# Graph attention on one core: sixteen late key tiles in place of twelve, every block of them moved by DMA, and a new order of PE's work in a step

## The reference

```
h = relu(layernorm(x))
q, k, v = h @ Wq[head], h @ Wk[head], h @ Wv[head]            # per head, 4096 x 64
scores = q @ k.T / 8 + 0.01 * eye - 1e16 * (1 - max(adj, eye))
out = x + sum over heads of softmax(scores) @ v @ Wo[head]
```

## Time and profile before

| what | value |
|---|---|
| time, median of three runs | 3127.58 us |
| span of the profiled execution | 3131.2 us |
| PE busy | 3056.8 us (98%) |
| DVE busy | 2444.3 us (78%) |
| ACT busy | 2171.6 us (69%) |
| POOL busy | 492.8 us (16%) |
| TensorE granted clock, mean | 0.992 |

### The profile page before, as it was taken

The page is one execution under the profiler, slowest core; times in us unless marked ns, Lnnn a source line. Parts: engine busy times, 40 slices in busy tenths (PEclk is TensorE's granted clock), DMA queues, the critical chain, the costliest instruction groups (busy, mean ns, idle before and its releaser), DMA issues.

```text
span 3131.2 us, 58791 instructions
## 1 busy us (share of the span) xinstructions
PE 3056.8 (98%) x18368; PEld 1892.8 (60%) x18368; DVE 2444.3 (78%) x4345; ACT 2171.6 (69%) x3297; POOL 492.8 (16%) x658
## 2 busy tenths in 40 slices
PE   7999999999999999999989999999999999999998
PEld 5566666666666666666556655666665666565664
DVE  6778788887878887887557877878877778777775
ACT  3677777777777777777547767767777667677675
POOL 3011111101111110111001111111111111111110
PEclk9999999999999999999999999999999999999999
DMA  5234444433444443344424433444433444433442
GB/s 154 53 85 88 95 79 98 84 81 78 91 91 84 94 85 85 73 95 87 94 74 80 88 84 73 87 93 81 93 79 72 86 94 81 93 79 72 89 93 52
DMA packets 217847, 267.82 MB, mean 86 GB/s; under 512 B 57472, under 2 KB 176768, under 8 KB 217728
## 3 DMA queue, kind: packets, MB, share of 16 engines
q1 hardware_dynamic: 173568, 178.51, 24.6%
q0 software_dynamic: 41984, 83.91, 16.1%
q10 hardware_dynamic: 2176, 4.19, 0.4%
HBM read 169.87 MB, written 12.71 MB: 58 GB/s over the span
## 4 chain that ended last, share of the span: by engine, by line
PE 92%; DVE 3%; issue 3%; DMA 1%; SPq 1%; DVEq 0%; ACT 0%; POOL 0%; POOLq 0%
PE psS L383 31%; PE psO L406 23%; PE psT L396 21%; PE psO L417 10%; PE psP L368 2%; PE psS L341 2%; DVE S L631 1%; PE psP L426 1%; PE psO L356 1%; PE psP L356 1%; DVE PT L645 1%; DMA S<-in_x 1%; SPq L239 0%; DMA S<-hT_scratch 0%; PE psT L327 0%
## 5 line engine op out<-in xcount | busy, mean ns | idle before, releaser
L631 DVE CUSTOM_DVE_ANT_0 S<-psS,B 128x1024 f32<-128x1024 f32 x1024 | 1239.6, 1211 | 169.0 <-PE psS L383 151.5
L517 ACT ACTIVATE S<-S,negm 128x1536 f32<-128x1536 f32 (+1 forms) x768 | 1094.8, 1427 | 62.9 <-DVE negm L638 59.7
L524 ACT ACTIVATE PT<-psT 128x512 f32<-128x512 f32 x768 | 457.0, 595 | 656.0 <-PE psT L396 654.3
L406 PE MATMUL psO<-PT,V 128*64 128x256 f32 x5120 | 836.0, 405 | 0.0
L396 PE MATMUL psT<-ident,S 128*128 128x128 f32 x5120 | 797.6, 283 | 31.4 <-DVE PT L645 24.3
L396 PEld LDWEIGHTS psT<-ident,S 128*128 128x128 f32 x5120 | 566.2, 141 | 398.2 <-issue 293.6
L383 PE MATMUL psS<-K,QH 128*128 128x512 f32 x2048 | 738.3, 442 | 8.4 <-DVE mx L631 5.9
L383 PE MATMUL psS<-K,QL 128*128 128x512 f32 x2048 | 643.8, 395 | 0.0
L645 DVE COPY PT<-psT 128x512 f32<-128x512 f32 x512 | 352.7, 689 | 332.4 <-PE psT L396 292.1
L658 DVE STREAM_TRANSPOSE S<-S 128x1536 f32<-128x1536 f32 x256 | 454.0, 1773 | 38.0 <-PE psO L417 37.9
L406 PEld LDWEIGHTS psO<-PT,V 128*64 128x64 f32 x5120 | 254.1, 135 | 362.4 <-issue 248.6
(11 more groups left out here) (52 smaller groups left out, 1056.1 us busy)
## 6 DMA issues: line engine op xcount, KB each, us to landing
S<-S SPq DMA_DIRECT2D x1536, 96.0 KB, 2.2
B<-in_adj POOLq DMA_DIRECT2D x256, 256.0 KB, 5.4
hq<-hT_scratch SPq DMA_DIRECT2D x32, 256.0 KB, 3.2
RB<-rden_scratch SPq DMA_DIRECT2D x128, 64.0 KB, 3.2
S<-in_x SPq DMA_DIRECT2D x8, 512.0 KB, 3.6
hT_scratch<-S ACTq DMA_DIRECT2D x8, 512.0 KB, 4.1
acc<-in_x POOLq DMA_DIRECT2D x16, 256.0 KB, 4.5
partial_scratch<-res POOLq DMA_DIRECT2D x16, 256.0 KB, 3.2
```

What stands on the lines that cost most here:

```text
L406: last = nc.tensor.matmul(psO[a * KD:(a + 1) * KD, 0:QW], V[:, 2 * s + a, h * KD:(h + 1) * KD], PT[:, s % RING, a * QW:(a + 1) * QW], star ...
L517: nc.scalar.activation(part, part, ACT.Exp, bias=negm[:, h % 2, q:q + 1], accum_out=sums[:, h % 2, q, e:e + 1]).then_inc(probs_ready, 1)
L524: nc.scalar.activation(PT[:, s % RING, :], psT[s % 2][:, :], ACT.Copy).then_inc(pt_act, 1)
L631: nc.vector.tensor_tensor_reduce(out=part, in0=psS[j % 2][:, :], in1=B[:, q, k * SLOT:(k + 1) * SLOT], scale=SCALE, scalar=LOWEST, op0=ALU ...
```

## The change

- `LATE` goes from 12 to 16, so the early key tiles go from 20 to 16: `TS` from 10 slots to 8, `SUBSTEPS` from 5 to 4. Each late transpose is 2048 columns wide instead of 1536, each move carries 2048-byte rows instead of 1536-byte ones, and `T1(h)` now fills all 4096 columns of query tile 1 in the other half. The first slot that waits for `late_moved` is slot 4 instead of slot 5 (`t1_first_slot`).
- All 16 quadrant blocks are moved by SP's DMAs (`MOVES` = 16); ACT's `copy_late` is gone.
- ACT takes all 8 slots; DVE takes none.
- PE's substep is: transposes 2c, transposes 2c + 1, scores c + 2, values 2c - 2, values 2c - 1. After the four substeps: scores 6, values 6 and 7, scores 7, late values of 6 tiles, scores 0 of the head after next, late values of 10 tiles, scores 1 of the head after next.
- DVE's list: mask 2, 3 and 4 in substeps 1, 2 and 3, then mask 5, then (even steps) both `query_lo`, then masks 6 and 7. The denominators stay in substep 2, ahead of mask 4.
- At the change of group, SP's weight loads also wait for the very last late values.

```diff
-LATE = 12
+LATE = 16
-MOVES = QUAD * (QUAD - 1)
+MOVES = QUAD * QUAD
-ACT_SLOTS = [0, 2, 4, 6, 8, 9]
-DVE_SLOTS = [1, 3, 5, 7]
+LATE_SPLIT = 6
+def t1_first_slot():
+    return SPT + (N - QT * LATE * P) // SLOT
 # wait_taken
-        slots, taken, start = (ACT_SLOTS, pt_act, PT_START) if s % TS in ACT_SLOTS else (DVE_SLOTS, pt_dve, 0)
-        engine.wait_ge(taken, count(i, h, len(slots), slots.index(s % TS) + 1 + start - (len(slots) if s < 0 else 0)))
+        engine.wait_ge(pt_act, count(i, h, TS, s + 1 + PT_START))
 # sync_program, at the change of group
         load(0, 0)
+        if not norm:
+            sp.wait_ge(late_used_before, STEPS)
 # sync_program, step
                 for qj in range(QUAD):
-                    if qi != qj:
-                        src, dst = late_blocks(h, qi, qj)
-                        sp.dma_start(dst, src).then_inc(late_moved, 16)
+                    src, dst = late_blocks(h, qi, qj)
+                    sp.dma_start(dst, src).then_inc(late_moved, 16)
 # tensor_program, step
             for c in range(SUBSTEPS):
                 transposes(i, h, 2 * c)
+                transposes(i, h, 2 * c + 1)
                 if nxt:
                     scores(i1, h1, c + 2)
...
                 if c:
                     values(i, h, 2 * c - 2)
-                transposes(i, h, 2 * c + 1)
-                if c:
                     values(i, h, 2 * c - 1)
...
             if nxt:
+                scores(i1, h1, SLOTS - 2)
+            values(i, h, TS - 2)
+            values(i, h, TS - 1)
+            if nxt:
                 scores(i1, h1, SLOTS - 1)
-            values(i, h, TS - 2)
+            values_late(i, h, range(LATE_SPLIT))
             if nxt2:
                 scores(i2, h2, 0)
-            values(i, h, TS - 1)
-            values_late(i, h)
+            values_late(i, h, range(LATE_SPLIT, LATE))
             if nxt2:
                 scores(i2, h2, 1)
 # scalar_program, step
-                if c in (1, 2):
-                    copy_late(i, h, (2 * c - 2, 2 * c - 1))
-                if 2 * c + 1 in ACT_SLOTS:
-                    take_slot(i, h, 2 * c + 1)
+                take_slot(i, h, 2 * c + 1)
 # vector_program, mask
-            if j == SPT + 1 and not first:
+            if j == t1_first_slot() and not first:
                 dve.wait_ge(late_moved, count(i, h, 16 * MOVES, 0))
-                dve.wait_ge(late_copied, count(i, h, QUAD, 0))
 # vector_program, step
-                if 2 * c + 1 in DVE_SLOTS:
-                    take_slot(i, h, 2 * c + 1)
...
-                if nxt2 and h % 2 == 0 and c > QUERY_AT:
-                    query_lo(i2, h2, c - QUERY_AT - 1)
+            if nxt:
+                mask(i1, h1, SUBSTEPS + 1)
+            if nxt2 and h % 2 == 0:
+                query_lo(i2, h2, 0)
+                query_lo(i2, h2, 1)
```

More of the change, by code:

```diff
@@ L128, in group_programs @@
     (bias_conv, bias_ready, q_proj, q_hi, q_lo, scores_ready, slot_masked, row_ready, probs_ready,
-     transposed, pt_act, pt_dve, pt_free, o_ready, projected, summed, den_ready, head_added,
-     late_transposed, late_moved, late_copied, late_used, odd_copied, o_summed, rden_stored, rden_in) = (
+     transposed, pt_act, pt_free, o_ready, projected, summed, den_ready, head_added,
+     late_transposed, late_moved, late_used, odd_copied, o_summed, rden_stored, rden_in) = (
         sem(f"{s}{g}") for s in (
             "bias_conv", "bias_ready", "q_proj", "q_hi", "q_lo", "scores_ready", "slot_masked", "row_ready",
-            "probs_ready", "transposed", "pt_act", "pt_dve", "pt_free", "o_ready", "projected", "summed", "den_ready",
-            "head_added", "late_transposed", "late_moved", "late_copied", "late_used", "odd_copied", "o_summed",
+            "probs_ready", "transposed", "pt_act", "pt_free", "o_ready", "projected", "summed", "den_ready",
+            "head_added", "late_transposed", "late_moved", "late_used", "odd_copied", "o_summed",
             "rden_stored", "rden_in"))
@@ L408, in values, with values_late @@
             last.then_inc(pt_free, 1)
-        def values_late(i, h):
-            pe.wait_ge(late_moved, count(i, h, 16 * MOVES, 16 * MOVES))
-            pe.wait_ge(late_copied, count(i, h, QUAD, QUAD))
+        def values_late(i, h, tiles):
+            if tiles[0] == 0:
+                pe.wait_ge(late_moved, count(i, h, 16 * MOVES, 16 * MOVES))
             PTL = S[:, h % 2, :, LC:N].rearrange("p q (i m a) -> p m q i a", i=QUAD, a=32)
-            for m in range(LATE):
+            for m in tiles:
                 half_ = m % 2
@@ L418, in values_late @@
                                         PTL[:, m, :, :, :], start=False, stop=(m >= LATE - 2))
-            last.then_inc(late_used, 1)
+            if tiles[-1] == LATE - 1:
+                last.then_inc(late_used, 1)
         def project(i, h):
@@ L524, in take_slot @@
             nc.scalar.activation(PT[:, s % RING, :], psT[s % 2][:, :], ACT.Copy).then_inc(pt_act, 1)
[L526 to L531, removed]
         def step(i, h, nxt, nxt2, prev):
@@ L639, in mask @@
                                         negate=True).then_inc(row_ready, 1)
[L641 to L645, removed]
         def transpose_late(i, h, q, before):
```

## The result

The changed kernel takes 3781.93 us (median of four runs, 3777.96 to 3784.8), the one before 3127.8 us beside it: a ratio of 1.209, with a 95% interval of 1.207 to 1.211. I had forecast 3487 us and a range of 3335 to 3590. The direction and the loop were right, the size was not: the loss is 654 us and not 360, and the measured time lies above the range.

The account below looks back on a forecast made before the run. The loop from late values through transpose, moves and landing to mask 4 was to replace PE as bound: 3131.2 + 255 (longer steps) + 95 (clock) + 10 (edges) = 3491 us span, 3487 us predicted, range 3335 to 3590.

Parts of the forecast that it names:

- the loop: Late values, transpose, 16 moves, landing, mask 4, scores 6: sets the step, mean 24.35 us, 1.62 more than before.
- the landing: Time until a move's data arrives: larger moves land 0.1 us later, bounds 0 and 0.4.
- the estimate beside it: Trainium skill's fixed 2.0 us plus bytes over 436 GB/s: a move lands 0.08 us later than before.
- PE's list: PE's work in a plain step, with fewer transposes and output-width changes: 2.0 us shorter, 19.8 us.
- rival 2: Moves land early enough, so PE stays the bound and the kernel gets faster: 2882 us; chance 0.08.
- Costs that no row shows directly: Additions to the loop: larger moves, adjacency crowd, edges; a step 2.02 us longer in all (255 us), edges 10 us.
- part (b): Adjacency loads beside the moves in one of four steps: 1.2 us there, 0.3 in the mean, bounds 0 and 1.0.
- The clock: PE runs slowly after its gap before scores 6: 1.5 us in each odd step, none in even ones, 95 us.
- the rule of the Trainium skill: Clock is halved after idle gaps between matmul bursts: odd steps pay, even ones do not; speaks against the change.
- the fourth: Rival: clock falls in every step (3619 us), or larger moves cost more, issue interval 0.73 us (3657 us); chance 0.11.

Follow-up runs that it names:

- e9: Changed kernel plus 14 unused matmuls in PE's gap, and without loading or converting adjacency after the first pair of each group: 3452.52 us.
- e1: Changed kernel with the late transposes' scratch in its own region instead of in `S`, so masks no longer wait for moves: 3038.84 us.
- e7: Kernel before with PE's order alone changed, plus ACT taking slot 1 and DVE slot 9 in exchange: 3044.79 us.
- e2: Changed kernel without loading and converting the adjacency after the first pair of each group: 3602.95 us.
- e3: Changed kernel with 14 matmuls that nobody reads put in PE's gap before the scores of slot 6: 3624.98 us.
- e5: Kernel before with PE's order alone changed: transposes and values of two slots together, late values split in 2 and 10 tiles: 3180.62 us.
- e6: Changed kernel with its 16 moves issued from two queues, eight by SP and eight by POOL, whose list is reordered: 3583.76 us.

## Why the prediction was wrong in size

*The loop: right.* The forecast was 24.35 us for the mean step, or 24.45 with 0.1 for the landing. (A move lands 2.4 us after its issue instead of 2.2, so 0.2 later, where the sum had 0.1 and the estimate beside it 0.08.) e9, which has neither adjacency crowd nor lost clock, runs h = 1 and 3 in 24.7 and 24.6, medians of 24.4. That the loop is the cause is shown by e1, which cuts it and takes 743 us off.

*PE's list: right.* 20.66 us by the same prices for e7's list, 20.66 measured. For the changed kernel's own list I had 19.8. e1 shows a median of 20.5 in h = 1, because ACT's exponentials between its first two slot copies hold PE's fourth slot some 0.7 us. I had put that at one us, but only into the arrival at the gap and not into rival 2.

*The step that failed: "Costs that no row shows directly", its part (b).* I gave 1.2 us to the crowd in one of four steps, with bounds of 0 and 1.0 us in the mean. Measured (e2) it is 6.1 us in h = 2, clock included, so 1.5 in the mean, above my upper bound. Of the 6.1, 5.2 are the later landing: from the first move to the mask it is 17.5 us in h = 2 and 12.3 in quiet steps, and without the loads (e2) 12.3 in h = 2 too. The mistake is visible in the earlier trace rows: I took the share of 0.52 for the moves' load, but that window also held the tail in which the last moves only land. Its 9.93 us x 0.52 = 5.2 us of all engines for 12 moves of 96 KB scale by 16/12 and by 4/3 to 9.2 us, and 9.3 were measured. That is not 0.7 of the 10.2 us of issue but nine tenths of it. So there is little room beside it.

The crowded window fits this: 0.86 x 17.81 = 15.3 us of engine time, 9.3 for the moves and 6 for the rest. Its 175 GB/s are 3.12 MB, 1.02 MB more than the moves carry, which is four adjacency loads of 256 KB (the kernel issues three in the window and one 1.6 us before it). The queue of POOL on the two pages gives the price of one: without 240 of the loads its share falls from 13.6% of 3780.6 us to 2.4% of 3606.8 us, 428 us or 1.8 us for each. The pages of the changed kernel and of e2:

```profile
q0 software_dynamic: 41984, 83.91, 13.6%
```

```profile
q0 software_dynamic: 7424, 20.98, 2.4%
```

By these prices, worked out from quiet steps and whole pages, an estimate is 9.3 + 4 x 1.8 + 2.4 of landing = 18.9 us from the first move to the mask. Measured are 17.77; the same estimate for a quiet step is 11.7 where 12.27 were measured. So the sum is good to about 1 us.

*Same step, left out:* h = 0 has the store of the result and the load of `acc` beside its moves, and its mask starts 14.4 us after the first move where quiet steps have 12.3. With the gap filled it is 2.2 to 2.5 us longer than its quiet neighbours (27.03 against 24.82 and 24.50). I had given this step nothing. No run takes these two transfers away, so that they are the cause is read from the timeline and not shown by itself.

*The clock: mechanism right, term too small.* I took 1.5 us in odd steps and none in even ones. e3 gives 2.0 to 2.1 in odd steps, and 0.9 in h = 0, where I had expected a gap of 1.4 us; with its crowd it is 4.1. In h = 2 the gap is 7.2 and PE is slow behind it as well. This term hangs on the one before it: a late landing makes the gap.

By the trace the rule of the Trainium skill that I had weighed (TensorE: Matmul & The Clock Gate, its table on why this matters) agrees in its direction: the granted clock of 0.901 rises to 0.971 when the gaps are filled, and to 0.990 in e9.

The sum: four steps were forecast at 102.0 us and took 112.84. The miss of 10.8 us is 3.5 in h = 0, 0.95 in h = 1, 5.8 in h = 2 and 0.6 in h = 3. Thirty-two times that is 347 us. Two last pairs without adjacency loads take some 11 off; 46 stood in my starting point instead (four steps of the kernel before take 92.35 in the mean, with long ones in the second group, where I counted 90.9). That leaves 290 us, and the span was missed by 290.

Of the rivals the fourth came nearest, at 0.11, and not by its own working. Its first half, a clock that falls in every step, is close to what the trace shows, but its price gave 3619 us. Its second half, larger moves that cost more, had put the cost into an issue interval of 0.73 us; SP issues one each 0.64 us as before, and the cost is the crowd at the engines. Rival 2, PE as the bound, would have needed e1's separate scratch.

What stays open: the last 0.9 of h = 2's 6.1 us is put down to the clock by subtraction only, since a filling that is long enough there was not tried. Nor is it shown what the store and the load cost h = 0, and why h = 0 is longer in the second group of some kernels.

## What to carry to other kernels

Before a buffer is widened so that it overlaps more of what another engine writes next, walk the loop once with times: when does the last reader let go, and who is queued behind the wait. A transfer is free only until a loop runs through it: four more moves cost 20 us here in the old schedule (some 40 without the luck in h = 0) and 517 us in the new one. Size a crowd by adding the engine time of everything that shares it (share x window), and do not compare a share that was read over a window with its tail to the stretch of issue alone. Such a sum was good to about 1 us here. And price PE's order by its changes of output width: here that gave a step to 0.01 us, but two slots asked for together need two copies that are not queued behind long work (e5 against e7).

## What was not expected of the hardware

Two queues moved 2 MB in 128-KB moves hardly faster than one (0.5 us of 12.3): each move took 5.4 us to land instead of 2.4, and 16 of them took 9.5 us of all engines' time instead of 9.3 (e6). And PE's clock is worth money even in a kernel that waits: 3.5 us of useless matmuls in each step made it 157 us faster (e3).
